# Heads behind experts: `between_m` moved to the end of each step of the shared loop

## Chip, cores and metric

One core of one Trainium2 chip (trn2). The metric is the time of the kernel on the device in microseconds, as the median of the runs shown.

## The reference

Four layers in a row over x of shape (4, 1024, 128), float32. Each is `x = x + layernorm(layer(layernorm(x)))`: an RWKV block, a mixture of experts with grouped routing (layer 2), a linear attention with decaying memory (layer 3), and a grouped-query attention with a second mixture of experts. The change touches the place where layers 2 and 3 overlap. What they compute, cut to that:

```python
# layer 2: 16 experts of width 64 and a shared one of width 128
g = silu(einsum('th,efh->tef', x, w1_e)); u = einsum('th,efh->tef', x, w3_e)
routed = einsum('tef,ehf,te->th', g * u, w2_e, combine)
shared = (silu(x @ w1_s.T) * (x @ w3_s.T)) @ w2_s.T

# layer 3: 16 heads of width 8, two memories each
q, k, v = (x @ Wq), (x @ Wk), (x @ Wv)            # q, k: rope, then elu(.) + 1
beta = clip(sigmoid(x @ Wbeta + bbeta), 0.001, 0.999)
M = M * b_t[:, :, None, None] + (k_t[:, :, None] * v_t[:, None, :])[:, None]
Z = Z * b_t[:, :, None] + k_t[:, None, :]
num = einsum('bd,bcde->be', q_t, M); den = einsum('bd,bcd->b', q_t, Z) + EPS
```

## The kernel before

Each engine has its own program, written out by hand, and the programs meet through semaphores alone. There is no queue beyond the order in which each engine's program issues its instructions, so that order is what a change can move.

**Layer 2** is cut into 8 groups of 512 tokens (`g`) times 9 weights (`j`: eight pairs of routed experts and the shared one), 72 units `n = 9 * g + j`. For a unit, PE does the gate matmul (L413, bank 4 for late units) and the up matmul (L416, bank 6), ACT does silu (`silu_m`, L1425), DVE multiplies the two (`gated_m`, L983), POOL multiplies by the routing weight (L1748, whose factor SP's DMAs bring in), and three units later PE multiplies by w2 (`out_m`, L428). Banks 4 and 6 are single for late units: gate waits for silu of the unit before, up waits for L983 of the unit before.

**The head of layer 3**, per group, is spread over 14 slices `k`, of which one runs with each unit number `v` (`head_slices(v)`, with `HEAD_AT[g] = max(16, 9 * g + 13)`). It belongs to what each engine calls `between_m(v)`; `between_m` also holds the close of a group of layer 2 (statistics `stats_m`, `add_m`, `rstd`). For a slice `k` of group `g`: 2 the statistics (DVE L745, L749); 5 the normalisation on ACT (L1308); 6 the transpose on PE (L310) and its copy on ACT (L1445); 7 to 10 a projection on PE (L452) and its multiply by the rope table on DVE (L1000, which empties the bank), with the sum of both halves on DVE at 8 and 10 (L1004) and then exp and relu on ACT (L1449, L1451); 9 and 11 the close of elu + 1 on DVE (L1012); 11 and 12 the decay projection on PE (L457) and tanh on ACT (L1457); 12 and 13 scale and clip on DVE (L1017, L1019). For `v >= 27` all of a head's results on PE use one bank, 7.

**The memories of layer 3** are 36 scans `n` (4 batches times 8 value columns and the normaliser), one a step of the loop over `C_STEPS` (39 steps). For a step PE makes the value (`value_c`, L501), DVE multiplies it by the key (`value_c`, L1070) and runs two scans over 1024 tokens (`memory_c(n, 0)` and `(n, 1)`, L1090), POOL adds the two memories (L1774) and multiplies by the query (L1776), and PE sums over the key dimension (`query_c`, L512 and L520). Value of step n + 1 waits for the second scan of step n.

In the first 27 steps of that loop two units run beside each scan:

```python
def beside(step):
    return [v for v in (ALONE + 2 * step, ALONE + 2 * step + 1) if v < MOE_STEPS]
```

with `ALONE = 36` and `MOE_STEPS = 90`. Units from 72 on have no expert work left apart from the last out matmuls, only slices of heads. At the end of a step the passes of layer 4's input (`pass_f`, L1112, L887, L1125 and others) and `weight_c` (L1099, L1101) follow.

Of the kernel before, what the change touches and what calls it, by code (L numbers as in the profile page):

```python
# [63 lines left out]
def build(nc, I, out):  # L64
    ctx = ExitStack()
    with ctx:
# [189 lines left out]
        FIRST_UNIT = 20  # L256
# [9 lines left out]
        def beside(step):  # L266
            return [v for v in (ALONE + 2 * step, ALONE + 2 * step + 1) if v < MOE_STEPS]
# [10 lines left out]
        def head_slices(step):  # L278
            return [(g, step - HEAD_AT[g]) for g in range(NG) if 0 <= step - HEAD_AT[g] < HEAD_SLICES]
# [21 lines left out]
        def tensor_program():  # L301
# [108 lines left out]
            def gate_up_m(n):  # L410
                g, j = divmod(n, 9)
                i = gate_bank(n)
                pe.matmul(room(i), w1[:, j, :], cf(XF, g), start=True, stop=True).then_inc(s["g_m"], 1)  # L413
                banks.lend(i, s["si_m"], n + 1)
                i = up_bank(n)
                pe.matmul(room(i), w3[:, j, :], cf(XF, g), start=True, stop=True).then_inc(s["u_m"], 1)  # L416
                banks.lend(i, s["a_m"], n + 1)
# [22 lines left out]
            def head_d(v, g, k):  # L440
                if k == 6:
                    pe.wait_ge(s["hn0"], 16 + g + 1)
                    i = next_d(v)
                    turned(room(i), lambda j: quarter(row(8 + g % 2), j), s["tp0"])
                    banks.lend(i, s["xf_d"], g + 1)
                    bank_of["turn_d", g] = i
                if 7 <= k < 11:
                    if k == 7:
                        pe.wait_ge(s["xf_d"], g + 1)
                        pe.wait_ge(s["w_ww"], 16)  # L450
                    i = next_d(v)
                    pe.matmul(room(i), wq4[:, k - 7, :], cf(XF, g), start=True, stop=True).then_inc(s["pj_d"], 1)  # L452
                    banks.lend(i, s["t_d"], 4 * g + k - 6)
                    bank_of["pj_d", g, k - 7] = i
                if 11 <= k < 13:
                    i = next_d(v)
                    pe.matmul(room(i), wbr[:, k - 11, :], cf(XF, g), start=True, stop=True).then_inc(s["pj_d"], 1)  # L457
                    banks.lend(i, s["beta_d"], 2 * g + k - 10)
                    bank_of["pj_d", g, k - 7] = i

            def experts(v):
                if v == 2:
                    cut_n(0)
                    cut_n(1)
                if 0 <= v - 3 < 9 * NG:
                    out_m(v - 3)
                if 9 <= v < 11:
                    cut_n(v - 7)
                if 18 <= v < 22:
                    cut_n(v - 14)  # L470
                if v < 9 * NG:
                    gate_up_m(v)

            def between_m(v):
                for g, k in head_slices(v):
                    head_d(v, g, k)

            for step in range(NG + 15):
                for lag, stage in ((15, gate_n), (14, turn_n), (10, ret_b), (9, vv_b), (8, kc_b), (4, turn_b), (2, res_b)):
                    if 0 <= step - lag < NG:  # L480
                        stage(step - lag)
                if step == FIRST_UNIT:
                    pe.wait_ge(s["w_wm"], 48)
                if step >= FIRST_UNIT:
                    experts(step - FIRST_UNIT)
                    between_m(step - FIRST_UNIT)
            for v in range(NG + 15 - FIRST_UNIT, ALONE):
                experts(v)
                between_m(v)


            def value_c(n):
                b, j = divmod(n, 9)
                i = VALUE[n]
                if j:
                    room(i)
                    room(i + 1)
                    if j == 1:
                        pe.wait_ge(s["xf_d"], 2 * b + 2)
                    for h in range(2):  # L500
                        ins = pe.matmul(bank(i + h), wvr[:, j - 1, :], cf(XF, 2 * b + h), start=True, stop=True)  # L501
                    ins.then_inc(s["vr_c"], 1)
                for h in range(2):
                    banks.lend(i + h, s["m_c"], n + 1)
# [28 lines left out]
            def weight_c(b, h, step):  # L533
                pe.wait_ge(s["wx_c"], b + 1)
                i = next_f(step)
                turned(room(i), lambda j: quarter(WX[:, :], 4 * h + j), s["wt_c"])
                banks.lend(i, s["wc_c"], 2 * b + h + 1)
                bank_of["weight", b, h] = i
# [52 lines left out]
            for step in range(C_STEPS):  # L591
                if 0 <= step - 2 < 36:
                    query_c(step - 2)
                for v in beside(step):
                    between_m(v)
                    experts(v)
                if step < 35:
                    value_c(step + 1)
                if step % 9 in (4, 5) and step < 36:
                    weight_c(step // 9, step % 9 - 4, step)  # L600
                for b, k in pass_slices(step):
                    pass_f(b, k, lambda: next_f(step))
# [137 lines left out]
        def vector_program():  # L740
# [231 lines left out]
            def gated_m(n):  # L972
                g, j = divmod(n, 9)
                dve.wait_ge(s["si_m"], n + 1)
                dve.wait_ge(s["u_m"], n + 1)
                if j == 8:
                    dve.wait_ge(s["o_m"], n - 2)
                    to = row(5 + n % 3)
                else:
                    if 8 * g + j >= 2:  # L980
                        dve.wait_ge(s["b_m"], 8 * g + j - 1)
                    to = row(3 + j % 2)
                dve.tensor_tensor(to, row(n % 3), bank(up_bank(n)), ALU.mult).then_inc(s["a_m"], 1)  # L983
# [49 lines left out]
            def between_m(v):  # L1033
                if 0 <= v - 3 < 9 * NG and (v - 3) % 9 == 8:
                    stats_m((v - 3) // 9)
                if 3 <= v < 9:
                    next(routes[1], None)
                    next(routes[1], None)
                if 9 <= v < 11:
                    spread_n(v - 7)  # L1040
                if 11 <= v < 18:
                    next(routes[2], None)
                    next(routes[2], None)
                if 18 <= v < 22:
                    spread_n(v - 14)
                for g, k in head_slices(v):
                    head_d(g, k)
# [100 lines left out]
            for step in range(C_STEPS):  # L1148
                units = [v for v in beside(step) if v < 9 * NG]
                if step < 36:  # L1150
                    value_c(step)
                    memory_c(step, 0)
                for v in beside(step)[0:1]:
                    between_m(v)
                for v in units[0:1]:
                    gated_m(v)
                if step < 36:
                    memory_c(step, 1)
                for v in beside(step)[1:2]:
                    between_m(v)  # L1160
                for v in units[1:2]:
                    gated_m(v)
                if step % 9 == 2 and step < 36:
                    weight_c(step // 9)
                for b, k in pass_slices(step):
                    pass_f(b, k)
# [124 lines left out]
        def scalar_program():  # L1291
# [168 lines left out]
            def experts(v):  # L1460
                if v == 3:
                    score_n(2)
                if 0 <= v - 3 < 9 * NG and (v - 3) % 9 == 8:
                    copy_m((v - 3) // 9)
                if v < 9 * NG:
                    silu_m(v)

            def between_m(v):
                for g, k in head_slices(v):
                    head_d(g, k)  # L1470
                if 0 <= v - 5 < 9 * NG and (v - 5) % 9 == 8:
                    add_m((v - 5) // 9)
# [87 lines left out]
            for step in range(C_STEPS):  # L1560
                for v in beside(step):
                    experts(v)
                    between_m(v)
                if step < 35:
                    value_c(step + 1)
                if step % 9 == 3 and step < 36:
                    spread_c(step // 9)
                if step % 9 in (4, 5) and step < 36:
                    weight_c(step // 9, step % 9 - 4)
                for b, k in pass_slices(step):  # L1570
                    pass_f(b, k)
# [470 lines left out]
```

## Time and profile before

| | us |
|---|---|
| median of 3 runs | 1546.14 |
| lowest, highest | 1541.69, 1546.69 |
| time of the profiled execution | 1541.69 |
| its span, first to last instruction | 1540.3 |
| mean granted TensorE clock of the span | 0.878 |
| busy in the span: PE, DVE, ACT, POOL | 1185.7, 1129.7, 734.5, 704.0 |

The time holds 1.4 us around the span. Busy shares of the whole span mix stages with different limits; the loop in question runs from about 366 us to about 785 us, the steps with two units in them from 366 to 710 us.

### The profile page before, as it was taken

To read this page: it belongs to the slowest core of one execution; us is meant where nothing else is said; L and a number is where in the kernel's file an instruction comes from. 1 tells how busy PE (TensorE), PEld (TensorE's weight loads), DVE (VectorE), ACT (ScalarE), POOL (GpSimd) and SP (SyncE) were. 2 spreads that over 40 slices of the span, in tenths; PEclk is the share of its full clock that TensorE was granted. 3 is DMA by queue.
4 is the path that set the end of the run, shared out by engine and by line. 5 is a ranking of instruction groups with operands and counts; after the bars stand their busy time and mean duration, and the time that the engine had idled before them with its cause. 6 is when DMAs were issued, how large, how long until landed. Compare 5 with 4: busy or idle time off the path is not lost.

```text
span 1540.3 us, 18685 instructions
## 1 busy us (share of the span) xinstructions
PE 1185.7 (77%) x5568; PEld 543.4 (35%) x5568; DVE 1129.7 (73%) x3003; ACT 734.5 (48%) x1599; POOL 704.0 (46%) x857
## 2 busy tenths in 40 slices
PE   3514986999998886657658678898989898988863
PEld 1212454555444443223222222333333333333322
DVE  5888645757988898578959786787888788876022
ACT  4634783255443253123230366656565656565641
POOL 7434672456777776438550122133412441335144
PEclk9856998999999996687875698999999999999995
DMA  3000104222111100004235101111020202000010
GB/s 107 0 1 0 46 1 108 80 77 62 35 48 42 35 14 0 0 4 63 43 51 78 20 1 30 32 17 35 4 33 15 37 4 33 4 1 3 1 42 14
DMA packets 33666, 47.02 MB, mean 31 GB/s; under 512 B 5007, under 2 KB 18191, under 8 KB 33263
## 3 DMA queue, kind: packets, MB, share of 16 engines
q1 hardware_dynamic: 30974, 43.84, 13.4%
q10 hardware_dynamic: 2592, 2.00, 0.5%
q8 instruction: 44, 0.72, 0.2%
q14 instruction: 56, 0.46, 0.1%
HBM read 39.14 MB, written 6.68 MB: 30 GB/s over the span
## 4 chain that ended last, share of the span: by engine, by line
PE 31%; DVE 21%; ACT 6%; issue 4%; POOL 4%; DMA 0%; ACTq 0%; DVEq 0%; POOLq 0%
PE PS L658 8%; PE PS L616 5%; PE PS L641 5%; DVE PS L1175 4%; DVE SS L1178 4%; PE PS L703 3%; DVE RB L1090 2%; PE PS L501 2%; PE PS L310 2%; ACT RB L1580 2%; DVE st L745 1%; ACT RB L1587 1%; DVE B L1090 1%; DVE PS L1070 1%; PE PS L520 1%
## 5 line engine op out<-in xcount | busy, mean ns | idle before, releaser
L1580 ACT ACTIVATE RB<-PS 128x512 f32<-128x512 f32 (+3 forms) x768 | 328.1, 497 | 265.7 <-PE PS L641 261.8
L616 PE MATMUL PS<-B 96*128 96x512 bf16 (+3 forms) x768 | 259.1, 360 | 55.6 <-DVE B L1221 24.2
L1829 POOL TENSOR_SCALAR_AFFINE_SELECT RB<-RB 128x512 f32<-128x512 f32 x128 | 81.3, 635 | 410.8 <-ACT RB L1580 410.8
L1175 DVE CUSTOM_DVE_ANT_0 PS<-PS,w_msk 128x128 f32<-128x128 f32 (+3 forms) x512 | 243.4, 503 | 29.1 <-PE PS L616 28.6
L641 PE MATMUL PS<-B 96*128 96x512 bf16 (+3 forms) x768 | 241.5, 336 | 18.6 <-ACT RB L1580 16.8
L1178 DVE TENSOR_REDUCE SS<-PS 128x1 f32<-128x512 f32 x256 | 175.2, 684 | 37.0 <-PE PS L616 36.1
L658 PE MATMUL PS<-RB,B 128*32 128x512 f32 (+3 forms) x1536 | 170.8, 517 | 14.4 <-ACT RB L1587 14.4
L616 PEld LDWEIGHTS PS<-B 96*128 96x128 bf16 x768 | 77.0, 101 | 204.8 <-DVE SS L1175 65.5
L1748 POOL TENSOR_TENSOR RB<-RB,B 128x512 f32<-128x512 f32 x64 | 82.6, 1292 | 92.9 <-DVE RB L983 68.1
L501 PE MATMUL PS<-B,WW 128*128 128x512 f32 x128 | 82.2, 776 | 37.6 <-DVE RB L1090 26.6
L641 PEld LDWEIGHTS PS<-B 96*128 96x128 bf16 x768 | 75.6, 100 | 99.1 <-ACT RB L1580 59.3
L1425 ACT ACTIVATE RB<-PS 128x512 f32<-128x512 f32 x72 | 42.8, 596 | 132.1 <-PE PS L413 132.1
L428 PEld LDWEIGHTS PS<-B,RB 128*128 128x128 f32 x576 | 77.9, 199 | 46.8 <-issue 28.6
L1647 POOL TENSOR_TENSOR rs<-rs,mhalf 128x4 f32<-128x4 f32 (+1 forms) x68 | 89.4, 1315 | 5.7
L428 PE MATMUL PS<-B,RB 128*128 128x128 f32 x576 | 79.5, 283 | 13.0 <-POOL RB L1748 12.9
L310 PE MATMUL PS<-w_ident,RB 128*128 128x128 f32 x256 | 46.3, 313 | 47.6 <-issue 21.5
L983 DVE TENSOR_TENSOR RB<-RB,PS 128x512 f32<-128x512 f32 x72 | 48.8, 679 | 41.6 <-PE PS L416 15.4
L413 PE MATMUL PS<-B 128*128 128x512 f32 x144 | 77.2, 619 | 1.3 <-ACT RB L1425 1.3
L416 PE MATMUL PS<-B 128*128 128x512 f32 x144 | 75.2, 604 | 2.4 <-DVE RB L983 2.4
L1175 DVE DVE_READ_ACCUMULATOR2_ANT SS<- 128x1 f32 x512 | 71.6, 140 | 0.0
L1774 POOL TENSOR_TENSOR RB<-RB 128x1024 f32<-128x1024 f32 x16 | 38.1, 2381 | 67.0 <-DVE RB L1090 67.0
L703 PE MATMUL PS<-WW,B 128*128 128x512 f32 x128 | 64.9, 635 | 2.2 <-DVE SS L1175 2.2
(243 smaller groups left out, 2229.3 us busy)
## 6 DMA issues: line engine op xcount, KB each, us to landing
B<-scrW SPq DMA_DIRECT2D x128, 128.0 KB, 3.0
B<-scrQ SPq DMA_DIRECT2D x72, 128.0 KB
scrQ<-B SPq DMA_DIRECT2D x6, 384.0 KB, 6.4
B<-scrK SPq DMA_DIRECT2D x36, 64.0 KB
X<-in_x SPq DMA_DIRECT2D x8, 256.0 KB, 8.5
out_dram<-X SPq DMA_DIRECT2D x8, 256.0 KB, 3.0
B<-in_w SPq DMA_DIRECT2D x3, 576.0 KB, 4.8
B<-in_zeros SPq DMA_DIRECT2D x9, 128.0 KB
```

The costliest lines, as they stand in the source:

```text
L428: ins = pe.matmul(quarter(p, q), quarter(row(5 + n % 3), q), w2[:, j, :], start=(j == 0 and q == 0), stop=(j == 8), skip_group_check=True)
L501: ins = pe.matmul(bank(i + h), wvr[:, j - 1, :], cf(XF, 2 * b + h), start=True, stop=True)
L616: pe.matmul(p[:, 0:w], qs[u % 3][:, h, 128 * i:128 * i + 128], keys_of(u, h)[:, 512 * c:512 * c + w], start=True, stop=True).then_inc(s["m ...
L641: pe.matmul(p[:, 0:w], keys_of(u, 4 * kl + z)[:, 128 * kt:128 * kt + 128], qs[u % 3][:, 4 * kl + z, 512 * qc + off:512 * qc + 512], start= ...
L658: ins = pe.matmul(p[32 * j:32 * j + 32, off:off + w], VA[:, 8 * (u // 2) + kt, 2 * (u % 2) + kl, :], pb[:, j, 0:w], start=(kt == 0), stop= ...
L703: pe.matmul(room(i), quarter(cf(HB, g), k - 9), wE[:, 4 * half:4 * half + 4, :].rearrange("p e c -> p (e c)"), start=True, stop=True).then ...
L1175: ins = dve.tensor_tensor_reduce(p, p, msk[:, 512 - w:512], 1.0, LOWEST, ALU.add, ALU.max, MX[:, u % 2, i, h, c:c + 1])
L1178: ins = dve.tensor_reduce(MX[:, u % 2, i, h, c:c + 1], p, AX, ALU.max)
L1580: act.activation(RB[:, 4 * (step % 3) + z, 0:w], bank(bank_of["score", step, z])[:, 0:w], ACT.Exp).then_inc(s["ex2"], 1)
L1647: own.done(pool.tensor_tensor(R[:, s4, 0], R[:, s4, 3], mhalf[:, 0:count], ALU.pow))
L1748: pool.tensor_tensor(row(5 + n % 3), row(3 + j % 2), CW[m % 4], ALU.mult).then_inc(s["b_m"], 1)
L1829: pool.affine_select(out=pb, in_=pb, compare_op=ALU.is_ge, fill=0.0, base=0, pattern=[[0, 4], [1, 128]], channel_multiplier=-1).then_inc(s ...
```

## The change

The order of `between_m` against `experts` in the loop over `C_STEPS`, on three engines; POOL and SP are as they were.

- On PE, `between_m` is folded into the end of `experts`: a unit's head slice comes behind its out, gate and up matmuls, where in this loop it came ahead of them. In the loops ahead of it the order was that already.
- On DVE, both `between_m` of a step come behind both `gated_m`, where each stood ahead of its own unit's.
- On ACT, both `between_m` come behind both `experts`, where each stood behind its own.

```diff
@@ PE @@
                 if v < 9 * NG:
                     gate_up_m(v)
-
-            def between_m(v):
                 for g, k in head_slices(v):
                     head_d(v, g, k)
...
                 for v in beside(step):
-                    between_m(v)
                     experts(v)
                 if step < 35:
                     value_c(step + 1)
@@ DVE @@
                 if step < 36:
                     value_c(step)
                     memory_c(step, 0)
-                for v in beside(step)[0:1]:
-                    between_m(v)
                 for v in units[0:1]:
                     gated_m(v)
                 if step < 36:
                     memory_c(step, 1)
-                for v in beside(step)[1:2]:
-                    between_m(v)
                 for v in units[1:2]:
                     gated_m(v)
+                for v in beside(step):
+                    between_m(v)
                 if step % 9 == 2 and step < 36:
                     weight_c(step // 9)
@@ ACT @@
                 for v in beside(step):
                     experts(v)
+                for v in beside(step):
                     between_m(v)
                 if step < 35:
                     value_c(step + 1)
```

## Rows read from the trace of the kernel before

**Rows 1.** Windows, a step each: length; busy PE, PEld, DVE, ACT, POOL; clock; DMA.

```profile
375.38:386.83 11.45, 9.59 (x43) 5.67 (x42) 11.38 (x17) 4.77 (x7) 9.23 (x9) 1.00 0.17 48
386.83:399.01 12.18, 10.44 (x37) 5.41 (x36) 12.08 (x11) 7.52 (x11) 10.57 (x10) 1.00 0.14 43
...
410.31:419.57 9.26, 8.14 (x32) 4.38 (x32) 7.63 (x8) 3.33 (x7) 6.64 (x8) 1.00 0.10 29
...
430.60:442.66 12.06, 12.06 (x42) 6.32 (x42) 11.17 (x9) 5.02 (x6) 7.83 (x5) 1.00 0.13 43
...
455.29:465.40 10.11, 9.87 (x41) 5.53 (x39) 9.87 (x8) 3.01 (x5) 9.31 (x9) 1.00 0.18 52
487.05:502.63 15.58, 14.80 (x55) 8.87 (x55) 12.76 (x12) 6.55 (x10) 9.85 (x10) 0.89 0.13 35
516.72:527.61 10.89, 7.70 (x23) 3.54 (x22) 7.63 (x7) 2.73 (x6) 5.63 (x6) 0.84 0.11 24
557.81:568.85 11.04, 8.12 (x22) 4.45 (x23) 9.91 (x16) 8.34 (x16) 9.43 (x8) 0.74 0.00 1
568.85:581.91 13.06, 10.65 (x51) 6.68 (x50) 12.08 (x24) 5.37 (x11) 12.25 (x10) 1.00 0.01 1
672.33:689.01 16.68, 9.84 (x29) 5.13 (x28) 16.54 (x25) 3.26 (x14) 6.00 (x4) 0.80 0.00 0
700.00:710.09 10.09, 5.46 (x13) 2.09 (x11) 10.02 (x23) 1.72 (x2) 6.99 (x4) 1.00 0.45 81
```

**Rows 2.** DVE's lines, 366 to 722 us; last row one line's minimum/median/maximum ns.

```profile
L983 DVE TENSOR_TENSOR RB<-RB,PS 128x512 f32<-128x512 f32 x36 | 24.4, 677 | 13.3 <-ACT RB L1425 7.1 <-PE PS L416 6.1
...
L1004 DVE TENSOR_TENSOR RB<-RB 128x512 f32<-128x512 f32 x12 | 18.3, 1528 | 0.4
...
L1012 DVE SCALAR_TENSOR_TENSOR B<-RB 128x512 f32<-128x512 f32 x12 | 13.5, 1124 | 0.0
...
L1019 DVE TENSOR_SCALAR B<-B x6: 427/1440/2472, 406.1 to 702.6; 128x512 f32<-128x512 f32 x6
```

**Rows 3.** In order of time, inside step 6: start, duration, what.

```profile
433.51 0.69 DVE L1004 TENSOR_TENSOR RB<-RB 128x512 f32<-128x512 f32 x1
...
435.63 2.28 DVE L1090 TENSOR_TENSOR_SCAN B<-SS,PS 128x1024 f32<-128x1024 f32 x1
...
437.82 0.67 DVE L1000 TENSOR_TENSOR RB<-PS,B 128x512 f32<-128x512 f32 x1
437.98 2.36 POOL L1774 TENSOR_TENSOR B<-B 128x1024 f32<-128x1024 f32 x1 [0.92 <-DVE B L1090]
...
438.40 2.48 DVE L1012 SCALAR_TENSOR_TENSOR B<-RB 128x512 f32<-128x512 f32 x1
...
440.42 2.68 POOL L1776 TENSOR_TENSOR B<-B 128x1024 f32<-128x1024 f32 x1
```

**Rows 4.** In order of time, DVE and POOL at the end of step 17.

```profile
575.24 1.27 POOL L1748 TENSOR_TENSOR RB<-RB,B 128x512 f32<-128x512 f32 x1
575.63 1.17 DVE L1017 TENSOR_SCALAR SS<-SS 128x512 f32<-128x512 f32 x1
...
576.47 2.54 POOL L1774 TENSOR_TENSOR SS<-B 128x1024 f32<-128x1024 f32 x1
...
576.83 2.46 DVE L1019 TENSOR_SCALAR SS<-SS 128x512 f32<-128x512 f32 x1
```

**Rows 5.** In order of time, steps 7 and 13; in brackets idle before, and releaser.

```profile
448.91 0.69 DVE L983 TENSOR_TENSOR RB<-RB,PS 128x512 f32<-128x512 f32 x1 [2.66 <-ACT RB L1425]
...
452.30 0.86 DVE L745 BATCH_NORM_STATS2 st<-X 128x6 f32<-128x128 f32 x4
...
520.43 1.12 PE L416 MATMUL PS<-B 128*128 128x512 f32 x2 [2.03 <-DVE RB L983]
...
522.72 3.58 PE L501 MATMUL PS<-B,WW 128*128 128x512 f32 x4 [1.16 <-DVE B L1090]
...
526.35 1.23 DVE L1070 TENSOR_TENSOR PS<-B,PS 128x1024 f32<-128x1024 f32 x1 [3.19 <-PE PS L501]
```

More of the change, by code:

```diff
@@ L485, in tensor_program @@
                     experts(step - FIRST_UNIT)
-                    between_m(step - FIRST_UNIT)
             for v in range(NG + 15 - FIRST_UNIT, ALONE):
                 experts(v)
-                between_m(v)
             def value_c(n):
@@ L1158, in vector_program @@
                     memory_c(step, 1)
-                for v in beside(step)[1:2]:
-                    between_m(v)
                 for v in units[1:2]:
                     gated_m(v)
+                for v in beside(step):
+                    between_m(v)
                 if step % 9 == 2 and step < 36:
```

## Prediction

> **What bounds the kernel now.** I read the page first, then DVE's instructions by form for the stretch 366 to 722 us, then the stretch cut into its steps, then all engines in order of time through single steps, and last the chain. Only the loop over `C_STEPS` changes its order, and in it only steps 0 to 26, in which units 36 to 89 run, two a step. Call the first unit of a step v1, the second v2; S0 and S1 are the two scans, G1 and G2 the two multiplies of L983, V the multiply of L1070, B1 and B2 what `between_m` does for v1 and v2. DVE's order in a step is now V S0 B1 G1 S1 B2 G2.
>
> In step 1 DVE is busy 11.38 of 11.45 us, in step 2 12.08 of 12.18, in step 8 9.87 of 10.11; PE is as full in some of them (12.06 of 12.06 in step 6) [rows 1]. A row there runs from the start of S0 to the next S0; steps 3, 5 and 7 lie between the bounds of their neighbours. So a step is as long as DVE's own work plus what DVE waits. It waits 13.3 us ahead of G1 and G2, for ACT's silu and for PE's up matmul, in the whole stretch [rows 2].
>
> One more thing is paid inside DVE's instructions. L1004, the sum of the rotation, takes 0.69 us in one place and a mean of 1.53; L1012 0.67 and 1.12; L1019 0.43 at least and 1.44 at its median [rows 2, 3]. The long ones stand where POOL is in an add: L1012 starts at 438.40 while L1774 runs from 437.98 to 440.34, and ends at 440.88; POOL's L1776, which then waited for DVE, takes 2.68 instead of 2.36 [rows 3]. The two take turns: L1017 at 575.63 waits out L1748 (it ends at 576.51), POOL's L1774 gets in before L1019, and L1019 from 576.83 waits that out as well and takes 2.46 [rows 4]. The scans, V, G1, G2 and L1000 read one operand from PSUM and show no such long forms. I call the four lines with both operands (or the only one) in SBUF the shared kind: each of the heads 3 to 7 has eight of them (L1004 twice, L1012 twice, L1017 and L1019 twice each), head 2 eight also, 48 in the stretch. What they cost over their short form is now 12x0.84 + 12x0.45 + 12x1.01 = 27.6 us [rows 2].
>
> **The change, part by part.** It adds and removes no instruction, no DMA and no wait; SP's queue and POOL's keep their order.
>
> *PE.* H, the head's matmul, moves from in front of out, gate and up of its unit to behind them. The up matmul, which G1 waits for, comes up to one H (about 1.0 us, a matmul of the shape of the up's 1.12 [rows 5]) sooner. But H of v2 now stands behind up of v2 and in front of `value_c` of the next step, and it waits for bank 7, which B1 on DVE frees. What is queued behind it is value, query and the next unit; V waits for value.
>
> *ACT.* silu of v2 goes in front of the exponentials of v1. Now S1 on DVE hides those exponentials, so I take no gain for it. The stall of 2.66 us ahead of G1 in step 7 [rows 5] comes from the normalisation for the unit before, which ACT still does ahead of this silu; it stays, at 2.6 by the same chain.
>
> *DVE.* The order becomes V S0 G1 S1 G2 B1 B2. This is the part with a price. POOL's L1774 starts 0.16 us after S1 ends (437.82 and 437.98 [rows 3]), and POOL's two adds hold the stretch to 5 us after it. Now B1 sits between S0 and G1, where POOL is mostly done, and its shared instructions are short (L1004 0.69 [rows 3]); some of B2 start before POOL and win. Behind G2, 0.6 us after the end of S1, all of them lose.
>
> I work out a step as 2.2 + w + 0.6 + 2.2 (S0, wait w, G1, S1, by starts) + tail + 1.24 (V). In the tail, counted from S1's end, G2 ends at 0.6, POOL's first add at 2.5; a shared instruction waiting then runs, POOL's second add goes from its end for 2.4 us, the next shared one runs, then POOL's L1748 for 1.27, and so on. Uncontended pieces: L1000 0.6 [rows 3], shared 0.6 to 0.7 (L1017, L1019 0.35 to 0.4), statistics 1.1 (0.86 for the four L745 [rows 5], and the aggregates behind them). By the two k of head_d in a step:
>
> - (8,9), step 6: L1000 to 1.2, L1004 to 3.2, L1000 3.8, L1012 to 6.1 (POOL's second add till 5.5). 5.0 + 6.1 + 1.24 = 12.3 against 12.06 [rows 1]: +0.3; step 15 the same, so +0.6.
> - (10,11), steps 7 and 16: as above, and statistics 1.1: tail 7.2, with w 2.6 in step 7. 16.0 against 12.63, +3.4; 13.4 against 11.04, +2.4: +5.8. In step 7 B1 used to fill the start of the stall and no longer does.
> - (12,13), steps 8 and 17, four shared: 2.85, 5.7, 7.3, 7.7. No V follows. 12.7 against 10.11, +2.6; with 2.2 of statistics 14.9 against 13.06, +1.8: +4.4.
> - (7,8), steps 1 and 10: statistics 1.1, L1000 to 2.3, H of v2 from 2.5 for 1.0, L1000 to 4.1, L1004 to 5.6 behind the second add. 11.8 against 11.45, +0.4; in step 10 a wait of 0.5 goes, -0.2: +0.2.
> - (9,10), steps 2 and 11: L1012 to 3.1, L1000 3.7, L1004 6.2, then 1.2 for weight_c: 7.4. PE is 0.8 late for G1, because value was held by H. 14.4 against 12.18, +2.3; step 11, with w 3.2 and 0.5 of a pass, 17.4 against 15.58, +1.8: +4.1.
> - (11,12), steps 3 and 12: three shared, tail 7.5: 13.7 against 11.30, +2.4, and +2.5: +4.9.
> - (13), steps 4 and 13: two shared, 2.85 and 5.7: 11.9 against 9.26, +2.7; against 10.89, +1.05: +3.75. Here V used to wait for value, so part is hidden.
> - (6,7), steps 5 and 14: no shared ones; G1 comes sooner and the wait for value shrinks: -1.1 each, -2.2 (11.03 now [rows 1]; L983 waits 1.7 of it for PE).
> - steps 0 and 9: nothing.
>
> That is +21.6 for steps 0 to 17. In 18 to 26 there is no G, the order is V S0 S1 B1 B2, and long waits for the passes cover much. Step 24: S0 and S1 4.4, L1004 and L1012 done 6.1 later, 10.5, where that part takes 8.7 now (two scans 4.4, L1000 twice 1.2, L1004 0.6, L1012 2.4): +1.8 of its 16.68 [rows 1]. Step 25 +0.7, step 26 12.6 against 10.09: +2.5. Steps 19 to 22 have S1 sooner, which starts value or the pass sooner: -1.8 together. Sum of these +3.2.
>
> Total +24.8. The chain goes through DVE, value and POOL in this loop and on into the passes, so I let it all through. Against the profiled execution, 1541.7 (its span 1540.3 and 1.4 around it), that makes 1566.5. The median shown is 1546.1, 4.4 above it; I put the forecast near the middle, **1568 us**.
>
> The turn-taking can be weighed against the Trainium skill. Its page "SBUF — State Buffer", section "Who interferes with whom", says that the port pair shared by VectorE and GpSimd is held for a whole instruction by whoever issues first, and that the other blocks fully; the long L1012 of this trace [rows 3] agrees. It says nothing of who follows; read as DVE keeping the pair once it has it, the sum would be near nothing, by the turns seen here [rows 4] it is the one above.
>
> **The rivals.** (a) *The second add does not get in.* DVE pays one wait a step, the first. Then the tails are (8,9) and (10,11) 0.9 shorter, (12,13) 3.6, (9,10) 1.8, (11,12) and (13) 2.4, twice each: 24.0 of the 21.6 and about 3 of the rest: no change, 1540 to 1546. The turns at the end of step 17 speak against it [rows 4], but they are few and the gaps between DVE's instructions decide.
>
> (b) *Faster: the waits ahead of G1 and G2 go.* PE and ACT serve the experts first, and of the 13.3 us [rows 2] most could vanish, if the shared instructions cost after the change what they cost now, 27.6 us. That would be 1541.7 - 13.3 = 1528 to 1536. It decides if B's work falls where POOL happens to be idle, say because POOL's adds are late. Against it: POOL follows S1 at once in almost all steps.
>
> (c) *TensorE's clock falls in many steps.* In the longer steps PE waits some 2.5 us for G1, then for S1. In step 13 a gap of 2.03 us stood ahead of an up matmul; value then took 3.58 instead of 1.88, V waited 3.19, and the granted clock of the step is 0.84 [rows 1, 5]. If some eight steps more get that at 3 us each: 1566.5 + 24 = 1590. Against it: a step made long by DVE's tail hides a slow value (2.2 + 0.6 + 2.2 + 0.2 + 3.6 = 8.8 against 10.7). How often such a gap would do it, one step can't tell. The skill's page "TensorE: Matmul & The Clock Gate", section "A second HAM failure mode: psum-queue depth-cycling", tells of a kernel whose clock went up and down because TensorE idled a little between groups of matmuls; by that, this rival is the likelier.
>
> **How the numbers follow.** The forecast has 0.62 (its own range 1556 to 1580: half of each class off), (c) 0.14, (a) 0.13, (b) 0.11. What a measurement can tell here is about 0.3%, 4.6 us. Slower is the forecast and (c), 0.76; the same is (a), faster (b). The range leaves out (b) and a part of (a) below, and the far end of (c) above: 1545 to 1592.
>
> **What would show it.** In the changed kernel, in steps 0 to 26: L1012 at a mean near 2.0 us (1.12 now), L1004 near 2.0 (1.53), L1017 and L1019 near 1.9 (0.5 and 1.45); idle ahead of L983 not much under 13; the stretch from the first scan, 365.9, to 710 longer by about 25; everything after 800 us unchanged in length. I am wrong if these durations stay as they are, if DVE's second shared instruction of a step is short, or if V waits for value behind H of v2 in most steps (H would then be the cost, not the port).

## The result, and the profile after

| | before | after |
|---|---|---|
| median of 17 runs, us | 1536.67 | 1556.87 |
| lowest, highest | 1528.28, 1546.69 | 1551.59, 1564.85 |
| profiled execution, its span | 1541.69, 1540.3 | 1556.09, 1554.8 |
| granted TensorE clock | 0.878 | 0.875 |

The ratio of the means is 1.0119, 95% interval 1.0097 to 1.0141: slower by 18.3 us on 1536.7 (0.0119 x 1536.7). The two medians lie 20.2 us apart. The median of before is lower than in the three runs that stood ahead of the prediction. Its profiled execution reaches the first scan at 365.93 us, that of after at 359.43; so the two are compared from scan to scan here, not end to end. The profiled executions differ by 14.4 us: -6.5 ahead of the first scan, +17.9 in the loop, +3.0 behind it. The first and the last of these lie in code that the change leaves alone; in the profiles of all fourteen kernels here the first scan starts at 359 to 366 us.

The lines moved by 4 to 7: L983 of before is L978 of after, L1000 is L995, L1004 is L999, L1012 is L1007, L1017 is L1012, L1019 is L1014, L1070 is L1065, L1090 is L1085, L1425 is L1418, L1774 and L1776 are L1768 and L1770, L1748 is L1742, L501 is L497. Part 1 of the page of after, busy time of each engine:

```profile
PE 1189.6 (77%) x5568; PEld 543.2 (35%) x5568; DVE 1145.6 (74%) x3003; ACT 734.7 (47%) x1599; POOL 707.1 (45%) x857
```

DVE is busy 15.9 us longer with the same work (1129.7 before); PE 3.9, POOL 3.1. Windows of after, the steps 1, 2, 4, 8, 13, 24 and 26 that answer to [rows 1], and step 5, then steps 0 to 17 and 18 to 26 as wholes (length; busy PE, PEld, DVE, ACT, POOL; clock; DMA):

```profile
368.88:382.01 13.13, 10.51 (x37) 5.58 (x36) 10.71 (x16) 4.00 (x7) 12.25 (x13) 0.87 0.14 49
382.01:396.17 14.16, 11.46 (x43) 6.01 (x43) 12.45 (x12) 7.46 (x11) 9.49 (x7) 1.00 0.10 30
...
409.73:421.18 11.45, 9.12 (x37) 4.81 (x36) 11.38 (x7) 3.07 (x7) 6.72 (x7) 1.00 0.06 22
421.18:429.65 8.47, 7.79 (x30) 3.67 (x29) 8.43 (x15) 2.32 (x5) 6.12 (x7) 1.00 0.17 62
...
459.99:471.22 11.23, 11.23 (x48) 6.57 (x47) 10.49 (x8) 3.29 (x5) 6.84 (x6) 1.00 0.14 47
...
530.13:541.58 11.45, 8.21 (x24) 4.04 (x25) 11.38 (x8) 2.50 (x6) 6.22 (x4) 0.85 0.01 1
...
682.32:698.28 15.96, 10.26 (x29) 5.38 (x28) 15.00 (x25) 3.26 (x14) 6.00 (x4) 0.68 0.00 0
709.66:721.88 12.22, 7.19 (x14) 2.89 (x13) 12.15 (x23) 2.75 (x5) 7.20 (x3) 0.82 0.45 85
359.43:597.10 237.67, 198.30 (x697) 105.99 (x695) 202.23 (x257) 88.39 (x145) 166.50 (x130) 0.94 0.10 33
597.10:721.88 124.78, 76.80 (x179) 35.15 (x180) 98.43 (x130) 33.71 (x75) 65.66 (x54) 0.75 0.08 16
```

The same two wholes of before:

```profile
365.93:581.91 215.98, 187.86 (x697) 102.81 (x695) 191.84 (x257) 88.13 (x145) 163.95 (x130) 0.97 0.12 36
581.91:710.09 128.18, 82.39 (x176) 37.43 (x176) 92.47 (x130) 34.17 (x75) 64.57 (x54) 0.72 0.08 15
```

Steps 0 to 17, called the dense steps below, took 215.98 and take 237.67 us: +21.7. Steps 18 to 26 took 128.18 and take 124.78: -3.4. Steps 27 to 35 took 71.0 and take 70.6. Of the +21.7, 10.4 is DVE's busy time (191.84 to 202.23) and 11.3 is DVE's idle time (24.1 to 35.4). The prediction had nearly all of it as busy time. Step 2 shows the other half: DVE was busy 12.08 of 12.18 us and now is 12.45 of 14.16. Step 4 is the predicted kind, 11.38 of 11.45.

DVE's lines in steps 0 to 17 of after, which answer to [rows 2] (busy us, mean ns, then the idle time ahead and what ended it):

```profile
L978 DVE TENSOR_TENSOR RB<-RB,PS 128x512 f32<-128x512 f32 x36 | 24.3, 676 | 20.3 <-PE PS L416 12.0 <-ACT RB L1418 7.4 <-issue 1.0
L1065 DVE TENSOR_TENSOR PS<-B,PS 128x1024 f32<-128x1024 f32 x16 | 19.5, 1219 | 5.9 <-PE PS L497 5.8
L999 DVE TENSOR_TENSOR RB<-RB 128x512 f32<-128x512 f32 x8 | 11.7, 1465 | 0.3
L1007 DVE SCALAR_TENSOR_TENSOR B<-RB 128x512 f32<-128x512 f32 x8 | 11.6, 1446 | 4.0 <-ACT RB L1444 4.0
L995 DVE TENSOR_TENSOR RB<-PS,B 128x512 f32<-128x512 f32 x16 | 10.9, 680 | 3.8 <-PE PS L452 3.4
L1014 DVE TENSOR_SCALAR B<-B 128x512 f32<-128x512 f32 x4 | 7.7, 1918 | 0.1
L1012 DVE TENSOR_SCALAR B<-B 128x512 f32<-128x512 f32 x4 | 6.1, 1525 | 0.0
L1014 DVE TENSOR_SCALAR SS<-SS 128x512 f32<-128x512 f32 x4 | 5.8, 1443 | 0.1
L1012 DVE TENSOR_SCALAR SS<-SS 128x512 f32<-128x512 f32 x4 | 5.2, 1309 | 0.0
```

The six groups of the shared kind add up to 48.1 us (11.7 + 11.6 + 7.7 + 6.1 + 5.8 + 5.2); in before the same 32 instructions took 37.5. So +10.6, as much as all of DVE's extra busy time. The idle time ahead of G1 and G2 rose from 13.3 to 20.3. Two waits are new: 4.0 ahead of L1007 for ACT's exponentials, 3.8 ahead of L995, 3.4 of it for PE's projection (none before in these steps). V waits 5.9 in place of 8.9.

### The profile page after: what moved, and what is told of

It is laid out like the page before. It is cut to its first block, busy times and chain, and to the rows that moved or that the text cites. A ratio compares the mean times of both kernels' runs of the same rounds, so it can differ in the third digit from the quotient of the medians.

```text
span 1554.8 us, 18685 instructions
## 1 busy us (share of the span) xinstructions
PE 1189.6 (77%) x5568; PEld 543.2 (35%) x5568; DVE 1145.6 (74%) x3003; ACT 734.7 (47%) x1599; POOL 707.1 (45%) x857
## 4 chain that ended last, share of the span: by engine, by line
PE 30%; DVE 21%; ACT 6%; POOL 4%; issue 4%; DMA 0%; ACTq 0%; DVEq 0%; POOLq 0%
PE PS L653 8%; PE PS L611 5%; PE PS L636 5%; DVE PS L1168 4%; DVE SS L1171 3%; PE PS L698 3%; DVE RB L1085 3%; PE PS L310 2%; ACT RB L1574 2%; PE PS L497 2%; DVE st L740 1%; ACT RB L1581 1%; DVE PS L1065 1%; DVE B L1085 1%; PE PS L678 1%
## 5 line engine op out<-in xcount | busy, mean ns | idle before, releaser
L653 PE MATMUL PS<-RB,B 128*32 128x512 f32 (+3 forms) x1536 | 171.9, 520 | 14.4 <-ACT RB L1581 14.4
L1742 POOL TENSOR_TENSOR RB<-RB,B 128x512 f32<-128x512 f32 x64 | 84.8, 1328 | 98.4 <-DVE RB L978 77.2
L497 PE MATMUL PS<-B,WW 128*128 128x512 f32 x128 | 84.9, 800 | 32.8 <-DVE RB L1085 22.7
L1418 ACT ACTIVATE RB<-PS 128x512 f32<-128x512 f32 x72 | 42.8, 596 | 127.6 <-PE PS L413 127.5
L416 PE MATMUL PS<-B 128*128 128x512 f32 x144 | 77.3, 620 | 7.1 <-DVE RB L978 7.1
L978 DVE TENSOR_TENSOR RB<-RB,PS 128x512 f32<-128x512 f32 x72 | 48.7, 678 | 43.0 <-PE PS L416 19.8
L1639 POOL TENSOR_SCALAR rs<-mv 128x4 f32<-128x4 f32 (+1 forms) x68 | 21.7, 320 | 102.5 <-DVE mv L744 99.5
```

The costliest lines, as they stand in the source:

```text
L653: ins = pe.matmul(p[32 * j:32 * j + 32, off:off + w], VA[:, 8 * (u // 2) + kt, 2 * (u % 2) + kl, :], pb[:, j, 0:w], start=(kt == 0), stop= ...
L1742: pool.tensor_tensor(row(5 + n % 3), row(3 + j % 2), CW[m % 4], ALU.mult).then_inc(s["b_m"], 1)
```

## What the new waits look like

Step 1 of after in order of time (start, duration, what; in brackets idle before, and releaser). Bank 7 is emptied by DVE's L995, and PE's L452 of the second unit waits for that:

```profile
375.50 0.66 DVE L995 TENSOR_TENSOR RB<-PS,B 128x512 f32<-128x512 f32 x1
...
376.21 2.08 PE L452 MATMUL PS<-B,WW 128*128 128x512 f32 x2 [2.62 <-DVE RB L995]
...
378.08 2.63 PE L497 MATMUL PS<-B,WW 128*128 128x512 f32 x4
...
378.32 0.69 DVE L995 TENSOR_TENSOR RB<-PS,B 128x512 f32<-128x512 f32 x1 [2.17 <-PE PS L452]
...
380.75 1.23 DVE L1065 TENSOR_TENSOR PS<-B,PS 128x1024 f32<-128x1024 f32 x1 [0.19 <-PE PS L497]
```

PE stands idle for 2.62 us, because DVE reaches v1's L995 only behind S1, G2 and the statistics. Then DVE stands idle for 2.17, because its very next projection is the one that PE has only just been allowed to start. Value (L497), query and the next unit are queued behind L452, so the up matmul comes late for the next G1, which waits 0.90 us for it. The chain DVE, PE, DVE sits inside one tail. L452 and L497 are also longer than their 1.13 and 1.88 elsewhere: TensorE's granted clock is 0.50 from 376.20 to 378.30, behind the gap.

Step 4 is as the prediction drew it, every shared instruction losing one turn:

```profile
414.88 2.35 POOL L1768 TENSOR_TENSOR B<-B 128x1024 f32<-128x1024 f32 x1 [4.49 <-DVE B L1085]
...
415.29 2.23 DVE L1012 TENSOR_SCALAR SS<-SS 128x512 f32<-128x512 f32 x1
417.31 2.42 POOL L1770 TENSOR_TENSOR B<-B 128x1024 f32<-128x1024 f32 x1
417.55 2.46 DVE L1014 TENSOR_SCALAR SS<-SS 128x512 f32<-128x512 f32 x1
```

L1012 ends with POOL's first add (417.23 and 417.52), L1014 waits out the second (to 419.73). It is the turn-taking of [rows 4].

## The experiments

A ratio is that to the kernel before, with its 95% interval; the length of steps 0 to 17, which is the number behind it, is from the profiled execution, 216.0 before and 237.7 after. It has a scatter of its own: of the runs below, one has the old order in all these steps and takes 217.6, and one has the new order in all of them and takes 234.5. So two lengths that differ by 3 us or less are not told apart.

**One engine, two engines.** PE's edit alone, and PE's and ACT's.

```diff
 PE, both:
                 for v in beside(step):
-                    between_m(v)
                     experts(v)
+                    between_m(v)
 ACT, the second kernel only:
                 for v in beside(step):
                     experts(v)
+                for v in beside(step):
                     between_m(v)
```

> Only PE takes the new order (head slice behind up); DVE and ACT keep the old one. If the cost comes from DVE's order (the port and what waits for it), this does little: ratio to the kernel before 0.997 to 1.004, the mean of L1004, L1012, L1017 and L1019 as before (1.53, 1.12, 0.5, 1.45 us), and PE never waits more than 1 us for L1000. If the head slice behind up is itself the cost, the ratio is 1.006 or more.

Measured: 1.0007 [0.998, 1.0034]; steps 0 to 17 take 221.5, 5.5 more than before, and steps 18 to 26 take 122.3, 5.8 less.

> PE and ACT take the new order, DVE keeps the old one. If DVE's order is the cost: 0.997 to 1.005, and of the 18 us the last part of the change brings 14 or more. If the exponentials behind the second silu are a cost (L1012 of the second unit waits for L1451), DVE's idle ahead of L1012 rises from 0 to some 3 us and the ratio is up to 1.004 on that alone.

Measured: 1.0051 [1.0024, 1.0077]; 229.1. DVE's lines with PE's edit alone:

```profile
L986 DVE TENSOR_TENSOR RB<-RB,PS 128x512 f32<-128x512 f32 x36 | 24.2, 673 | 6.1 <-PE PS L416 3.7 <-ACT RB L1428 2.4
L1073 DVE TENSOR_TENSOR PS<-B,PS 128x1024 f32<-128x1024 f32 x16 | 19.5, 1220 | 12.2 <-PE PS L501 12.2
...
L1003 DVE TENSOR_TENSOR RB<-PS,B 128x512 f32<-128x512 f32 x16 | 10.9, 679 | 10.9 <-PE PS L452 10.9
```

The up matmul does come sooner by PE's edit: the wait ahead of G1 and G2 falls from 13.3 to 6.1. But DVE's old order wants the head's projection ahead of G1, and waits 10.9 for it, and V 3.3 more. ACT's edit adds 4.1 ahead of the elu's close (L1015 there, for the exponentials); here S1 does not hide them. So the orders of PE and ACT already cost 7.8 us (0.0051 x 1536.8) of the 18; I had expected DVE's order to bring nearly all of it. In both mixtures of orders DVE pays with waits that neither the old order nor the new one has to this extent.

**Where in the loop.** The whole change in steps 0 to 17 alone, and in 18 to 26 alone (each of the three edits under the condition `step < 18` or `step >= 18`, the old order in the other steps).

> The whole change, but only in steps 0 to 17, in which units still have expert work. By the two traces the stretch of these steps grew by 21.7 us, the rest shrank by 3.4: if the two parts are independent, 21 to 22 us over the kernel before, ratio 1.014. If the gain of the last nine steps was only slack that the late start of them gave, this gives the same as the whole change, 1.012.

Measured: 1.0127 [1.0082, 1.0172]; 234.5.

> The whole change, but only in steps 18 to 26, in which only head slices are left. If the two parts are independent: 3 to 4 us less than the kernel before, ratio 0.9975 (my step 'sum +3.2' of these steps was then of the wrong sign). If port waits rule here too, as the prediction had it: +3 us, 1.002. The stretch of these nine steps in the profile decides: 128.2 us before, 124.8 with the whole change.

Measured: 1.0033 [1.001, 1.0056]; steps 0 to 17 take 217.6, as they should with the old order. The dense steps bear the cost. In the steps from 18 on the expected gain of 0.9975 did not come: by time the edit there costs 1.5 to 8.6 us, which answers to the prediction's +3.2. By the profiles these steps are shorter all the same: 128.2 and 127.4 us in the two kernels that are the old one there, 124.8 and 124.7 in the two that are the new one, in windows with a granted clock of 0.71 to 0.75. What the nine steps seem to give is not found in the whole time, and no run here shows where it goes.

**The port side.** POOL's two memory operations on 32 of 1024 columns, in both orders. These kernels leave out most of the query's sum; they serve to give a wait a price.

```diff
-  pool.tensor_tensor(z, MEM[n][0], MEM[n][1], ALU.add)
+  pool.tensor_tensor(z[:, 0:32], MEM[n][0][:, 0:32], MEM[n][1][:, 0:32], ALU.add)
-  pool.tensor_tensor(z, z, batch(B[QD], b), ALU.mult)
+  pool.tensor_tensor(z[:, 0:32], z[:, 0:32], batch(B[QD], b)[:, 0:32], ALU.mult)
```

> The kernel before with POOL's two adds and multiplies of a step (L1774, L1776) cut to 32 of 1024 columns, so most of the query's sum is left out; instructions and semaphores stay. POOL then holds the shared side of SBUF for hardly any time. Port theory: the four shared lines fall to near their short forms (0.69, 0.68, 0.4, 0.43), 22 to 26 us of DVE time over steps 0 to 26, and the time falls by 15 to 25 us. If the long forms have another cause, they stay.

Measured: 0.9846 [0.9804, 0.9889]; 201.2. DVE's busy time in these steps falls by 19.2 us, 18.8 of it in the shared kind (37.5 to 18.7).

> The changed kernel with the same cut of L1774 and L1776. If the port were all of the change's cost, this equals the run before it (difference under 3 us). If, as the trace after suggests, half of the cost is DVE and PE waiting for each other at the end of a step (value behind the second head slice), it stays 8 to 12 us slower than that run.

Measured: 0.9898 [0.9873, 0.9923]; 213.3. Three of DVE's lines in steps 0 to 17 of the changed kernel with this cut:

```profile
L978 DVE TENSOR_TENSOR RB<-RB,PS 128x512 f32<-128x512 f32 x36 | 24.4, 679 | 16.1 <-PE PS L416 11.0 <-ACT RB L1418 4.7 <-issue 0.3
...
L995 DVE TENSOR_TENSOR RB<-PS,B 128x512 f32<-128x512 f32 x16 | 10.9, 680 | 4.3 <-PE PS L452 4.3
...
L1007 DVE SCALAR_TENSOR_TENSOR B<-RB 128x512 f32<-128x512 f32 x8 | 6.9, 861 | 4.3 <-ACT RB L1444 4.3
```

With the long POOL operations gone, the new order still costs 12.1 us in the dense steps (213.3 - 201.2). By whole time it costs 8 us (0.0052 x 1534), with intervals that overlap. My theory of the port as the whole cause falls here. The shared kind takes 18.7 us in the old order and 24.1 in the new one, for POOL's L1742 is still there. The waits ahead of L995 and L1007 stand as in after; the one ahead of G1 and G2 is 16.1 and hardly above the 15.5 of the old order with this cut.

**Value ahead of the second head slice.** On the kernel after: what is queued behind L452 of v2 is taken out of its way.

```diff
                 for v in beside(step):
                     experts(v)
+                    (between_m(v) for the first unit only)
                 if step < 35:
                     value_c(step + 1)
+                (between_m(v) of the second unit)
```

> The changed kernel with value_c of the next step moved on PE in front of the second unit's head slice. If value held behind that slice makes PE late for the next G1 and G2 (idle ahead of L983 rose from 13.3 to 20.3 us), 5 to 8 us of the 18 come back: ratio to the kernel before 1.006 to 1.009. If the port sets the length alone, nothing comes back: 1.011 to 1.013.

Measured: 1.0195 [1.017, 1.0221]; 238.2. V waits less (4.7), the wait for L452 grows (4.9), G1 and G2 wait as before the edit (19.7). Value was not what suffered: the wait for the bank stays where it was and the next unit is still behind it. The dense steps are as long as in after (237.7). By ratio this kernel is 12 us slower than after; 5.6 of that stand in steps 18 to 26 (130.4). Why there, and where the rest is, I can't tell.

**Shared slices ahead of S1.** On the kernel before: DVE does v2's slices from 8 on ahead of S1, when POOL is mostly idle.

```diff
                 for v in units[0:1]:
                     gated_m(v)
+                for v in beside(step)[1:2]:
+                    early_m(v)          # slices k >= 8 of between_m
                 if step < 36:
                     memory_c(step, 1)
```

> From the kernel before: on DVE the second unit's slices 8 to 13 move in front of the second scan, where POOL is mostly idle; PE and ACT as before. Port theory: the shared lines fall to near their short forms, 20 us of DVE time; but value starts after a later second scan, so V waits up to 1.5 us more a step, 15 us over 10 steps. 0.992 to 1.000. If waits for the head slice and for exp eat it: over 1.003.

Measured: 1.0175 [1.0144, 1.0205]; 225.8. DVE's lines of this kernel in steps 0 to 17:

```profile
L1076 DVE TENSOR_TENSOR PS<-B,PS 128x1024 f32<-128x1024 f32 x16 | 19.6, 1226 | 14.9 <-PE PS L501 14.9
...
L1004 DVE TENSOR_TENSOR RB<-RB 128x512 f32<-128x512 f32 x8 | 7.4, 926 | 0.3
L1012 DVE SCALAR_TENSOR_TENSOR B<-RB 128x512 f32<-128x512 f32 x8 | 5.8, 729 | 4.5 <-ACT RB L1459 4.5
```

The port side is as I said: away from POOL's adds L1004 falls from 1529 to 926 ns and L1012 from 1125 to 729. DVE's busy time falls by 11.1 us, and its idle time rises by 20.9. Of that rise V's wait for value makes 6.0 (14.9 in place of 8.9), for S1 comes later and value waits for S1. The exponentials make 4.5, scans that wait for POOL 3.0 (3.6 ahead of L1096, 0.6 before), and a pass's L1118 waits 5.2 for PE, where its wait was nothing. The short instruction is paid for with a late scan and what hangs on it.

**The bank freed early.** On the kernel after: v1's L995 goes right behind G1, ahead of S1; all else of `between_m` stays at the end. Then the same with POOL's operations cut as above.

```diff
                 for v in units[0:1]:
                     gated_m(v)
+                for v in beside(step)[0:1]:
+                    for g, k in head_slices(v):
+                        turn_d(g, k)      # L995 of the slice, nothing else of it
                 if step < 36:
                     memory_c(step, 1)
```

> The changed kernel, but the first unit's L1000 (which empties bank 7) stands right behind G1, ahead of the second scan; all else of the head stays behind G2. If the second head slice waiting on PE for bank 7, with value and the next unit behind it, is what makes the waits, then idle ahead of L1000 and ahead of G1 and G2 falls from 3.4 + 20.3 us to under 18 together over steps 0 to 17, and the stretch of these steps from 237.7 to 228 to 233 us. If only the port counts, the stretch stays within 2 us.

Measured: 1.0098 [1.0059, 1.0137]; 233.7, just outside the expected 228 to 233.

> The same, with POOL's L1774 and L1776 cut to 32 of 1024 columns, as in the two small runs (most of the query's sum is left out). Steps 0 to 17 took 201.2 us in the old order and 213.3 in the new with this cut. If the wait for bank 7 makes most of these 12.1 us, 202 to 207; if it is ACT's exponentials behind the second silu (L1012 waits 4.3 us for L1451), 208 or more.

Measured: 0.9754 [0.9717, 0.9792]; 201.6. DVE's lines in steps 0 to 17, first with POOL's full operations:

```profile
L978 DVE TENSOR_TENSOR RB<-RB,PS 128x512 f32<-128x512 f32 x36 | 24.2, 671 | 13.7 <-PE PS L416 8.4 <-ACT RB L1432 4.5 <-issue 0.6
...
L1010 DVE TENSOR_TENSOR RB<-RB 128x512 f32<-128x512 f32 x8 | 14.9, 1869 | 0.1
L1018 DVE SCALAR_TENSOR_TENSOR B<-RB 128x512 f32<-128x512 f32 x8 | 14.2, 1771 | 4.4 <-ACT RB L1458 4.4
L995 DVE TENSOR_TENSOR RB<-PS,B 128x512 f32<-128x512 f32 x16 | 10.9, 678 | 0.6
```

and with the cut ones:

```profile
L1010 DVE TENSOR_TENSOR RB<-RB 128x512 f32<-128x512 f32 x8 | 6.3, 789 | 0.1
L1018 DVE SCALAR_TENSOR_TENSOR B<-RB 128x512 f32<-128x512 f32 x8 | 5.6, 696 | 4.4 <-ACT RB L1458 4.4
```

This pair tells the two causes apart. One early multiply takes the wait for L452 away (3.8 to 0.6) and 6.6 of the wait ahead of G1 and G2 (20.3 to 13.7; the other kernel with the new order in these steps has 17.8). With POOL out of the way, the new order then costs 0.4 us in the dense steps (201.6 against 201.2), where it cost 12.1. The whole time agrees: 0.9754 against 0.9898, with intervals apart. It even lies below the 0.9846 of the old order with the cut, by some 14 us; 5.1 of them stand in steps 18 to 26 (112.9 against 118.0), the rest I can't place. The 4.4 ahead of the elu's close are still there in this kernel, so that wait can't be what cost the 12.1.

With POOL's adds the same edit brings 4.0 of 21.7, which is near the scatter of 3 us; by ratio it is 1.0098 against 1.0119, and the intervals overlap. The reason stands in DVE's lines: the shared instructions now start earlier, straight into POOL's adds, and the six groups take 55.4 us (48.1 in after), L1010 a mean of 1869 ns.

| steps 0 to 17, us | POOL in full | POOL cut |
|---|---|---|
| old order | 216.0 | 201.2 |
| new order | 237.7 | 213.3 |
| new order, bank freed early | 233.7 | 201.6 |

Of the 11.7 us that the bank brings in the right column (213.3 - 201.6), 6.9 are DVE's idle time and 4.8 its busy time; the shared kind falls from 24.1 to 20.7 in it. In step 1 of the changed kernel with the cut the granted clock is 0.87, behind a gap of 2.63 us ahead of L452, so a part of the 11.7 can be the clock's.

**The second product of the rotation left in PSUM.** On the kernel before: L1000 writes back into the bank it reads, and L1004 (L1008 here) reads it there, so that it has one operand in SBUF.

```diff
-  dve.tensor_tensor(row(q + half), bank(...), cs[...], ALU.mult)
+  dve.tensor_tensor(pj if half else row(q), pj, cs[...], ALU.mult)
-  dve.tensor_tensor(row(q), row(q), row(q + 1), ALU.add)
+  dve.tensor_tensor(row(q), row(q), pj, ALU.add)
 PE gets the bank back behind the sum in place of the product.
```

> From the kernel before, order untouched: the second product of the rotation (L1000 at k = 8 and 10) stays in its PSUM bank and L1004 reads it there, so that it has one operand in SBUF; the bank comes free 0.7 us later. If the port makes the long L1004, all 12 in steps 0 to 26 (16 in all) take about 0.69 us, 10 us less of DVE time; as the lines behind it may wait in its place, I expect 3 to 9 us: ratio 0.994 to 0.998. If the length of L1004 has another cause, its mean stays near 1.5 and the ratio at 1.000.

Measured, in 5 rounds: 0.9965 [0.9944, 0.9986], median 1530.60; 212.1. In order of time, first this kernel in step 1, then the kernel before at the same place:

```profile
375.29 2.37 POOL L1778 TENSOR_TENSOR SS<-B 128x1024 f32<-128x1024 f32 x1 [0.93 <-DVE B L1094]
375.83 0.69 DVE L1008 TENSOR_TENSOR RB<-RB,PS 128x512 f32<-128x512 f32 x1
376.44 0.68 DVE L986 TENSOR_TENSOR RB<-RB,PS 128x512 f32<-128x512 f32 x1
```

```profile
382.15 2.36 POOL L1774 TENSOR_TENSOR SS<-B 128x1024 f32<-128x1024 f32 x1 [0.92 <-DVE B L1090]
382.69 2.37 DVE L1004 TENSOR_TENSOR RB<-RB 128x512 f32<-128x512 f32 x1
...
384.98 0.68 DVE L983 TENSOR_TENSOR RB<-RB,PS 128x512 f32<-128x512 f32 x1
```

The sum starts 0.54 us into POOL's add in both and takes 0.69 in one, 2.37 in the other. The Trainium skill, page "SBUF — State Buffer", section "Who interferes with whom", says that a DVE instruction with at most one SBUF input, outside the perf modes that use two ports, does not contend with GpSimd; this row agrees. One input in SBUF is not enough by itself: L1019 (L1014 of after) has only one, and the row of step 4 above has it at 2.46 us beside POOL, against 0.43 at its shortest. The eight sums take 5.5 us in place of 12.2, 6.7 less, and the dense steps are shorter by 3.9: the other shared lines meet POOL more (L1012 of before 9.0 to 9.7, L1017 4.7 to 6.0).

**That, and the new order in steps 5 and 14.** They were the only dense steps shorter in after (8.47 and 8.68 against 11.03 and 11.03), so the kernel above got the new order in these two.

> The second product of the rotation in PSUM, as in the run before, and the new order on all three engines in steps 5 and 14 alone, where the units hold slices 6 and 7: no instruction of the shared kind, and no second head slice that waits for DVE. By the traces these two steps fall from 11.0 us each to 8.5 and 8.7, and the next ones keep their length: 5 us less than the run before, which was 0.9965 of the kernel before: 0.992 to 0.995. If the gain of the two steps is given back by the steps behind them, 0.996 to 0.998.

Measured, in 5 rounds: 0.997 [0.9949, 0.999], median 1529.71; 210.4. Steps 5 and 14 take 11.04 and 11.03 here. So the order in these two steps alone does not make them short. Steps 4 and 5 together took 20.29 us and take 19.92 in after, steps 13 and 14 together 21.92 and 20.13. My reading is that PE catches up in the longer step ahead. The kernel with the bank freed early fits it: its step 13 is as long as in after (11.44), but at a granted clock of 0.70, with 13 matmul records in place of 24, and its step 14 takes 11.00. No run tests that reading by itself. Both of the last two kernels beat the kernel before; between them the intervals don't tell.

## Why the prediction was right, and where its steps were not

The forecast was 1568 in 1545 to 1592, slower at 0.76. It came out slower, by 18.3 us where the sum had 24.8, and 1556.9 is just inside the likeliest case's own range. Of the 11 us to 1568, 5.0 are the starting point (1536.7 in place of 1541.7), 4.6 the sum (24.8 against 20.2 between the medians), and 1.5 what the forecast added on top. So the direction was right and its frame too, but the loss has two causes, where the prediction gave nearly all of it to one.

- **"So a step is as long as DVE's own work plus what DVE waits"**: held. For windows cut at DVE's own scans it is true by its form; it was the frame in which the loss could be found.
- **The sum for steps 0 to 17**, +21.6: measured +21.7, or 19.3 by the means of the two profiles that each order has. That it fits so well is partly luck, since its two halves were mis-sized against each other. By class, predicted and measured: (8,9) +0.6, +1.9; (10,11) +5.8, +6.4; (12,13) +4.4, +2.1; (7,8) +0.2, +3.4; (9,10) +4.1, +5.0; (11,12) +4.9, +4.1; (13) +3.75, +2.8; (6,7) -2.2, -4.9; steps 0 and 9 nothing, +1.1.
- **The shared kind's price** was oversized. I said means near 2.0 for L1012 and L1004 and 1.9 for L1017 and L1019; over steps 0 to 26 they are 1.45, 1.62, 1.35 and 1.77. By my means all 48 instructions would have cost 38.2 us more (12 x 0.47 + 12 x 0.88 + 12 x 1.38 + 12 x 0.45), some 25 of it in steps 0 to 17; they cost 18.6 more (55.5 to 74.1), 10.6 of it in steps 0 to 17. Part of the reason stands in the experiment on the bank: waits for PE and ACT push the shared instructions out of POOL's adds. With the wait for bank 7 gone they cost 55.4 in these steps, 17.9 more than before.
- **"H of v2 now stands behind up of v2 ... and it waits for bank 7"**: the mechanism was named, priced in class (7,8) at one H of 1.0 us and in (9,10) at 0.8, and held against me if V waited. It was undersized, and V was the wrong place to look: V waits less than before. The wait shows at L995 (3.8), at G1 by way of the up matmul (L416: 6.1 to 12.0), and at PE itself. This is the term that was mis-sized most: in the kernels with POOL's cut it is worth 11.7 us (213.3 - 201.6), with what it does to the shared lines and to the clock in it. My sign of being wrong, V waiting behind H, did not come (V's wait fell from 8.9 to 5.9), and yet H had a price of the same order as the port's.
- **"S1 on DVE hides those exponentials"**: it does not; DVE waits 4.0 us for them ahead of L1007. They now start behind both silu, and the close of the elu comes soon behind G2. What that wait costs in time is not shown: with the bank freed and POOL's cut it is 4.4, and the dense steps are only 0.4 longer than in the old order.
- **Idle ahead of L983 "not much under 13"**: it rose to 20.3. Rival (b), that it goes, is refuted for this kernel; PE's order alone brings it to 6.1, but DVE then waits 10.9 for the projection.
- **Steps 18 to 26**, +3.2: measured -3.4 (step 24 from 16.68 to 15.96, where I had +1.8; step 26 from 10.09 to 12.22, where I had +2.5), while the change in these steps alone makes the whole time longer by 1.5 to 8.6 us. By the profile the term has the wrong sign, by the time the right one; it stays open.
- **Rival (a)**, the second add doesn't get in: refuted, by the rows of step 4 above. **Rival (c)**, TensorE's clock, some 24 us more: refuted at that size. The granted clock of steps 0 to 17 went from 0.97 to 0.94, and the matmuls of PE in them from 187.9 to 198.3 us busy, so the clock has a share in the 21.7. In step 1 of after it is the likely reason of 1.5 of the 13.13 us: the kernel with the change in the first 18 steps, at a granted clock of 1.00, takes 11.63 there. Over all the dense steps that kernel has 0.96 and 234.5 us where after has 0.94 and 237.7. No run takes the clock away by itself.
- **Small things in the working.** S1 of step 6 ends at 437.91 (435.63 + 2.28); 437.82 is where the next instruction starts. The 27.6 us leave out L1017, which adds 1.5. Step 15 was taken to be like step 6, though it took 19.17 us and not 12.06; by class the two still came out near. The 0.8 by which PE is late was counted in step 2 and left out in step 11.

Two causes, then, that cover for each other: POOL's share of SBUF, and bank 7 emptied late by DVE. Shown by experiment are what each costs in the dense steps with the other taken away (bank 12.1 - 0.4, POOL's adds 17.7 - 0.4) and that both together cost 21.7, less than the 29.0 that these two prices add up to. The exponentials' wait is shown by its rows alone, in the seven kernels with the new order on ACT in the dense steps; taking it away by itself was not tried, nor was the PSUM edit on the new order. The price of the clock is open as well.

## What to carry to other kernels

When work is moved behind something, look at what the moved work sets free (here a bank), and not only at what the moved work costs where it lands; the engine that waits for it may be the one that feeds the mover. Two delays at one place don't add up: take them away together and one by one before either gets a price. A sum that read both operands from SBUF beside GpSimd's work could be given one operand in PSUM, which was the one edit here that paid (0.9965).

## What was not expected of the hardware

A gap on TensorE doesn't always bring its clock down. In step 1 of after PE idled 2.62 us ahead of L452, which then took 2.08 and value 2.63; the granted clock was 1.00 up to the gap and 0.50 from 376.20 to 378.30, the lower of its two levels (1.2 GHz in place of 2.4). The kernel with the change in the first 18 steps has the same gap at the same place, and a granted clock of 1.00 behind it, from 379.90 to 382.00:

```profile
379.94 1.13 PE L452 MATMUL PS<-B,WW 128*128 128x512 f32 x2 [2.62 <-DVE RB L1003]
380.90 1.88 PE L501 MATMUL PS<-B,WW 128*128 128x512 f32 x4
```

What else decided between the two, these rows don't show.
